# Splitting four fused weight products on GpSimd in place of VectorE, between ScalarE's eviction and the output product

## What is computed

```python
q = (hidden_states @ Wq).reshape(B, Sq, H, D)
k = (encoder_hidden_states @ Wk).reshape(B, Skv, H, D)
v = (encoder_hidden_states @ Wv).reshape(B, Skv, H, D)
q = rmsnorm(q, gq)
k = rmsnorm(k, gk)
scores = jnp.einsum('bqhd,bkhd->bhqk', q, k) * scale
attn = jax.nn.softmax(scores, axis=-1)
out = jnp.einsum('bhqk,bkhd->bqhd', attn, v)
return out.reshape(B, Sq, H * D) @ Wo
```

## Time and profile before

| | |
|---|---|
| median of three runs | 634.99 us |
| lowest and highest of them | 634.95, 635.37 us |
| span of the profiled execution, first to last instruction | 633.0 us |
| TensorE busy | 616.1 us, 97% of the span |
| VectorE busy | 489.0 us, 77% |
| ScalarE busy | 428.4 us, 68% |
| GpSimd busy | 231.0 us, 36% |

### The profile page before, as it was taken

How to read it: one execution, slowest core, us unless ns; L and a number is a source line. 1 busy time by engine, 2 the same in 40 slices (tenths; PEclk the granted TensorE clock), 3 DMA queues, 4 the chain that set the end, 5 groups by cost and what they waited for, 6 DMA issues and landing times.

```text
span 633.0 us, 11694 instructions
## 1 busy us (share of the span) xinstructions
PE 616.1 (97%) x3681; PEld 530.9 (84%) x3681; DVE 489.0 (77%) x1138; ACT 428.4 (68%) x1097; POOL 231.0 (36%) x275
## 2 busy tenths in 40 slices
PE   8888899999999999999999999999999999999997
PEld 5756678999999999999998888888887888887886
DVE  4999998777777678778867688788877777777776
ACT  5895999988888888879998544356444444444442
POOL 5677866766666666546664010000000000000000
PEclk9999999999999999999999999999999999999999
DMA  7420140100000000000012354444656466554640
GB/s 277 153 75 26 51 126 26 52 26 2 2 2 2 2 1 2 1 2 1 2 43 84 84 162 143 152 140 127 200 153 170 107 174 174 161 165 138 198 128 33
DMA packets 33509, 56.47 MB, mean 89 GB/s; under 512 B 12784, under 2 KB 13488, under 8 KB 33328
## 3 DMA queue, kind: packets, MB, share of 16 engines
q1 hardware_dynamic: 33456, 55.83, 29.3%
HBM read 53.45 MB, written 1.31 MB: 87 GB/s over the span
## 4 chain that ended last, share of the span: by engine, by line
PE 82%; DVE 8%; ACT 3%; issue 2%; POOL 2%; DMA 1%; SPq 0%; DVEq 0%; POOLq 0%; ACTq 0%
PE bank L286 24%; PE bank L288 23%; PE bank L287 23%; PE bank L834 4%; PE bank L809 2%; PE bank L801 2%; DVE w L1705 1%; DMA x<-in_x_tok 1%; DVE stats L1658 1%; DVE amax L1762 1%; POOL att L540 1%; ACT att L1341 1%; PE bank L716 1%; PE bank L868 1%; DVE w L1723 1%
## 5 line engine op out<-in xcount | busy, mean ns | idle before, releaser
L1380 ACT ACTIVATE inter_hi<-inter 128x512 fp32r<-128x512 f32 x63 | 39.8, 632 | 140.5 <-DVE inter L1940 140.5
L286 PE MATMUL bank<-xnT_hi,front_hi 128*128 128x512 f32 (+1 forms) x260 | 102.0, 392 | 0.0
L288 PE MATMUL bank<-xnT_hi,front_lo 128*128 128x512 f32 (+1 forms) x260 | 101.7, 391 | 0.0
L287 PE MATMUL bank<-xnT_lo,front_hi 128*128 128x512 f32 (+1 forms) x260 | 101.7, 391 | 0.0
L1944 DVE TENSOR_TENSOR inter_lo<-inter,inter_hi 128x512 fp32r<-128x512 f32 x63 | 43.6, 692 | 37.5 <-ACT inter_hi L1380 36.9
L1341 ACT ACTIVATE att<-bank,shift,rq 128x256 f32<-128x256 f32 x128 | 71.3, 571 | 0.0
L1829 DVE TENSOR_REDUCE rowmax<-bank 128x2 f32<-128x512 f32 x64 | 43.7, 685 | 27.4 <-PE bank L288 27.2
L540 POOL TENSOR_TENSOR att<-att,rowinv 128x512 f32<-128x512 f32 x60 | 62.1, 1054 | 5.2 <-DVE rowinv L1846 5.2
L524 POOL TENSOR_TENSOR rk<-msq,minus_half 128x4 f32<-128x4 f32 x32 | 33.1, 1035 | 78.7 <-DVE msq L1818 78.6
L1913 DVE TENSOR_TENSOR prod<-gate_s,bank 128x512 f32<-128x512 f32 x63 | 43.3, 687 | 21.9 <-PE bank L288 19.8
L287 PEld LDWEIGHTS bank<-xnT_lo,front_hi 128*128 128x128 f32 x260 | 48.9, 188 | 11.3
(11 more groups left out here) (273 smaller groups left out, 1843.3 us busy)
## 6 DMA issues: line engine op xcount, KB each, us to landing
w_all<-w_rows SPq DMA_DIRECT2D x128, 128.0 KB, 3.0
raw<-in_expert_w SPq DMA_DIRECT2D x32, 384.0 KB, 3.6
wvo_raw<-in_expert_w SPq DMA_DIRECT2D x16, 384.0 KB, 3.7
e_more<-in_expert_w SPq DMA_DIRECT2D x16, 384.0 KB, 3.6
raw<-in_head_qk SPq DMA_DIRECT2D x8, 384.0 KB, 3.6
wvo_raw<-in_head_vo SPq DMA_DIRECT2D x8, 384.0 KB, 3.2
gate_raw<-in_gate_wT SPq DMA_DIRECT2D x1, 1408.0 KB, 9.8
x<-in_x_tok SPq DMA_DIRECT2D x2, 512.0 KB, 6.1
```

The source lines that it names most:

```text
L286: pe.matmul(out, l_hi, r_hi_, start=start, stop=False, skip_group_check=True)
L287: pe.matmul(out, l_hi, r_lo_, start=False, stop=False, skip_group_check=True)
L288: return pe.matmul(out, l_lo, r_hi_, start=False, stop=stop, skip_group_check=True)
L1380: act.activation(inter_hi[:, slot, :], inter[:, slot, :], ACT.Copy).then_inc(a_Ihi, 1)
```

## The change

Head pairs 4 to 7 (`SPLIT = 4`) are treated another way. ScalarE's `whole_m(p)` scales the bank into `m_raw`, unrounded, at the place in its order where `high_m(p)` stood; `m_raw` shares its memory with `m_lo`. VectorE's four calls of `low_m` are gone. GpSimd's new `split_m(p)` stands in loop group g = p, behind `rms_q`: one instruction rounds `m_raw` into `m_hi`, GpSimd waits for it, and a second one writes the remainder over `m_raw`. TensorE's `output` waits for these pairs on the new count `g_Mlo`; the waits that protected the banks are now on `a_Mhi`, ScalarE's count.

```diff
@@ -29,6 +29,7 @@
 MAGIC = 12582912.0
 LOWEST = -3.0e38
 EARLY = 5
+SPLIT = 4
 LAST = 28
 GAIN = 127.0 / EPS
 
@@ -216,6 +217,11 @@
         back_hi = sc("back_hi", [P, PAIRS - EARLY, 768], F32R)
         back_lo = sc("back_lo", [P, PAIRS - EARLY, 768], F32R)
         cctx.close()
+        ectx = ExitStack()
+        ectx.enter_context(nc.sbuf_tensor("ahead_of_m", [P, 8704], F32))
+        m_whole = ectx.enter_context(nc.sbuf_tensor("m_whole", [P, PAIRS, 2, 2, HID], F32))
+        ectx.close()
+        m_raw = m_whole[:, :, 1, :, :]
         m_hi, m_lo = m_all[:, :, 0, :, :], m_all[:, :, 1, :, :]
 
         t_S, t_T, t_O, t_Y, t_Q, t_K, t_TQ, t_TK, t_M = (sem(n) for n in (
@@ -225,7 +231,8 @@
         v_max, v_shift_c, v_Tlo, v_Y, v_inv, v_Qlo, v_Klo, v_sqK, v_mk, v_mq, v_Olo, v_Mlo, v_gk = (
             sem(n) for n in ("v_max", "v_shift_c", "v_Tlo", "v_Y", "v_inv", "v_Qlo", "v_Klo", "v_sqK", "v_mk",
                              "v_mq", "v_Olo", "v_Mlo", "v_gk"))
-        g_rk, g_rq, g_kn, g_att, v_Wlo, g_Wlo = (sem(n) for n in ("g_rk", "g_rq", "g_kn", "g_att", "v_Wlo", "g_Wlo"))
+        g_rk, g_rq, g_kn, g_att, v_Wlo, g_Wlo, g_Mlo = (sem(n) for n in (
+            "g_rk", "g_rq", "g_kn", "g_att", "v_Wlo", "g_Wlo", "g_Mlo"))
 
 
         dctx = ExitStack()
@@ -539,6 +546,13 @@
                 a = att[:, n % 2, h, :, :]
                 pool.tensor_tensor(a, a, rowinv[:, n % 2, h, :].unsqueeze(2).broadcast_to([P, 2, SEQ]),
                                    ALU.mult).then_inc(g_att, 1)
+
+            def split_m(p):
+
+                pool.wait_ge(a_Mhi, p + 1)
+                link_g(pool, pool.tensor_scalar(m_hi[:, p, :, :], m_raw[:, p, :, :], 1.0, 0.0, ALU.mult, ALU.add))
+                pool.tensor_tensor(m_lo[:, p, :, :], m_raw[:, p, :, :], f(m_hi[:, p, :, :]),
+                                   ALU.subtract).then_inc(g_Mlo, 1)
 
             pool.wait_ge(pool_const, 5)
             pool.wait_ge(a_ctx, 1)
@@ -624,6 +638,8 @@
                     low_w(EARLY + 1, 2 * g)
                     pool.wait_ge(v_shift_c, g + 3)
                     low_w(EARLY + 1 + g, 1 - g)
+                if SPLIT <= g < PAIRS:
+                    split_m(g)
                 if g == 9:
                     pool.wait_ge(a_rw, 1)
                     pool.memset(f(r_both[:, 4 * LOGC:]), 0.0).then_inc(g_rw, 1)
@@ -851,7 +867,7 @@
                 b, p = g // PAIRS, g % PAIRS
                 pe.wait_ge(v_Olo, g + 1)
                 if b == 0:
-                    pe.wait_ge(v_Mlo, p + 1)
+                    pe.wait_ge(*((v_Mlo, p + 1) if p < SPLIT else (g_Mlo, p - SPLIT + 1)))
                 if p == 0 and h == 0:
                     wait(pe, v_Y, b)
 
@@ -1052,7 +1068,7 @@
             down(6, 7)
             down(7, 2)
             fuse_vo(6, 4)
-            pe.wait_ge(v_Mlo, 5)
+            pe.wait_ge(a_Mhi, 5)
             turn_rows_1(1, 5)
             pe.wait_ge(v_xB, 7)
             turn_q(1, 7)
@@ -1061,9 +1077,9 @@
             proj_q(3, 2, True)
             pe.wait_ge(c_u, 2)
             turn_rows_1(2, 5)
-            pe.wait_ge(v_Mlo, 6)
+            pe.wait_ge(a_Mhi, 6)
             fuse_vo(7, 6)
-            pe.wait_ge(v_Mlo, 7)
+            pe.wait_ge(a_Mhi, 7)
             turn_rows_1(3, 4)
             pe.wait_ge(v_Qlo, 2)
             proj_k(3, 7, True)
@@ -1073,7 +1089,7 @@
                 if g + 1 < GROUPS:
                     scores(g + 1)
                 if g == 0:
-                    pe.wait_ge(v_Mlo, 8)
+                    pe.wait_ge(a_Mhi, 8)
                 if g + 2 < GROUPS:
                     pe.wait_ge(a_sqQ, 4 * min(n, GROUPS))
                     turn_q(g + 2)
@@ -1351,6 +1367,11 @@
             def high_m(p, bk=KBK):
                 act.wait_ge(t_M, p + 1)
                 act.activation(m_hi[:, p, :, :], bank4(bk), ACT.Copy, scale=tg[:, 1:2]).then_inc(a_Mhi, 1)
+
+            def whole_m(p, bk):
+
+                act.wait_ge(t_M, p + 1)
+                act.activation(m_raw[:, p, :, :], bank4(bk), ACT.Copy, scale=tg[:, 1:2]).then_inc(a_Mhi, 1)
 
             def weight_exps(half):
                 act.wait_ge(v_shift, half + 1)
@@ -1490,26 +1511,26 @@
             square_q(1, 3)
             copy_q2(5, 6, 0)
             raw_q(2, 4)
-            high_m(4, 5)
+            whole_m(4, 5)
             square_q(2, 4)
             split_w(4)
             normalise_1(1)
             copy_q2(6, 4, 7)
-            high_m(5, 6)
+            whole_m(5, 6)
             copy_q2(7, 3, 2)
             normalise_1(2)
             exps(0, 0)
             exps(0, 1)
             copy_rows(1, 1, 5)
             act.wait_ge(a_h1, 7)
-            high_m(6, 4)
+            whole_m(6, 4)
             high_q(1, 7)
             high_k(1, 3)
             normalise_1(3)
             copy_rows(2, 2, 5)
             raw_q(3, 2)
             act.wait_ge(a_h1, 8)
-            high_m(7, 6)
+            whole_m(7, 6)
             copy_rows(3, 3, 4)
             raw_k(3, 7)
             square_q(3, 2)
@@ -2059,7 +2080,6 @@
             mean_q(1)
             stats_2(5)
             low_w(3)
-            low_m(4, 5)
             row_max(0, 0)
             row_max(0, 1)
             row_shift(0)
@@ -2071,14 +2091,11 @@
             row_inverse(0, 0)
             row_inverse(0, 1)
             low_rows(1, 1, 5)
-            low_m(5, 6)
-            low_m(6, 4)
             low_q(1, 7)
             low_k(1, 3)
             mean_q(2)
             low_rows(2, 2, 5)
             low_rows(3, 3, 4)
-            low_m(7, 6)
 
             for g in range(GROUPS):
                 n = g + 4
```

## The result

Four runs of the changed kernel gave 641.95, 640.19, 640.96 and 642.06 us, a median of 641.46 us, against 634.97 us for the kernel before beside them: a ratio of 1.0101 (95% interval 1.0088 to 1.0113), 6.5 us slower. The forecast was 640.3 us with a range up to 643.8. The spans of the four runs are 640.2 (the profiled one), 638.4, 639.2 and 640.0 us; their mean granted clocks, in the same order, 0.997, 1.0, 1.0 and 0.997. The forecast span was 638.4 us. So two of the runs agree with it to 0.8 us, and two, at a lower clock, are 1.6 and 1.8 us above it.

A forecast was written before the change was run, and what follows sets the result against it. TensorE was taken to bound the kernel, busy throughout loop groups 5 to 8. Late splits add 5.35 us and removing `low_m` nothing: 634.99 + 5.35 = 640.3 us, range 637.0 to 643.8 us.

The forecast's parts named there:

- The four `low_m` at nothing: Before the loop: removing VectorE's four passes, 2.9 us, gains 0, covered by ScalarE's program ahead of `turn_q(2)`.
- One sign: At the loop's start: group 0's `turn_q(2)` should start at 98.0 us as before, released by ScalarE.
- rival (d): Loop start: VectorE sets it, so the removed `low_m` give back up to 2.9 us; not slower, 635.9 us; chance 0.05.
- GpSimd's prices: In `split_m` on GpSimd: rounding 512 columns takes 0.62 us and the remainder 1.28 us.
- the sum worked out from it, 4.7 us: Groups 5 to 8: total loss if the remainder took the skill's 1.07 us instead of 1.28; 4.7 instead of 5.35 us.
- The stalls and how they add up: TensorE ahead of `output(g - 1, 0)`, groups 5 to 8: idle about 2.2, 0.95, 1.25 and 0.95 us, 5.35 in all.
- The rule itself: Groups 5 to 8: TensorE's lateness is the larger of its old lateness and 2.2 us plus GpSimd's lateness.
- The lateness of GpSimd: Groups 5 to 7: GpSimd late by 0.95, 2.2 and 3.15 us, through row inverses (1.25 us slack) or `msq`.
- rival (a): Groups 5 to 8: only the first stall costs, GpSimd's idle time absorbing the rest; 2.2 us, 637.2 us; chance 0.08.
- (c): Groups 5 to 8: each group pays in full, 4 x 2.2 = 8.8 us, 643.8 us; chance 0.05.
- Rival (b): Loop: GpSimd's remainder holds VectorE's `row_shift(6)` 0.85 us; if this came back in every group, 641.2 us; chance 0.10.
- Rival (e): Loop stalls: TensorE's clock falls; one group at half clock costs up to 8.1 us more, 648.5 us; chance 0.02.

The follow-up runs named there:

- e5_early_ahead: Changed kernel with GpSimd's split one loop group earlier and ahead of `rms_q` instead of behind it: 634.52 us, ratio 1.0000 to the kernel before.
- e6_dve4: e5_early_ahead with VectorE instead of ScalarE moving the four banks whole, at the places of the removed `low_m`: 633.91 us, ratio 0.9989 to the kernel before.
- e2_ahead: Changed kernel with each split in its own group but ahead of `rms_q`: 637.66 us, ratio 1.0043 to the kernel before.
- e3_pair7: Changed kernel with `SPLIT = 7`, so only pair 7 is split by GpSimd, pairs 4 to 6 as before: 638.23 us, ratio 1.0051 to the kernel before.
- e11_changed: The changed kernel again, unedited, beside e10_busy in the third set: 640.28 us, ratio 1.0090 to the kernel before.
- e1_early: Changed kernel with the split one loop group earlier, still behind `rms_q`: 635.51 us, ratio 1.0010 to the kernel before.
- e8_changed: The changed kernel again, unedited, in the second set, for its clocks: 641.25 us, ratio 1.0101 to the kernel before.
- e4_busy: Changed kernel with eight unused 512-column products filling TensorE's first stall, first set: 640.54 us, ratio 1.0095 to the kernel before.
- e10_busy: Changed kernel with the same fill of the first stall as e4_busy, third set: 640.31 us, ratio 1.0092 to the kernel before.

## Why the prediction held, and where it did not

**The four `low_m` at nothing: right.** The distance from `fuse_vo(4)` to `turn_q(2)`, 20.04 to 20.08 us with and without them, shows it in the traces, and e5_early_ahead shows it in the time, 634.52 beside 634.43 us. One sign was not as I wrote: the profile puts the idle time ahead of `turn_q(2)` down to "issue", not to ScalarE. That ScalarE's program is the cover is borne out twice: its last square ends 0.1 us ahead of `turn_q(2)` before, after and in e6_dve4, though that start moves, and e6_dve4 starts the loop 0.8 us sooner by taking passes off ScalarE and giving them to VectorE. So rival (d) falls.

**GpSimd's prices: right.** 0.62 and 1.27 us for 0.62 and 1.28. The floor of the Trainium skill (GPSIMD Engine Reference, 2.1 Instruction dispatch), by which the second would have lasted 1.07 us, is kept: 1.27 us lies above it. But the sum worked out from it, 4.7 us, is farther from the 5.6 us measured at clock 1.0 than 5.35 is.

**The stalls and how they add up: right.** Forecast 2.2, 0.95, 1.25 and 0.95 us, 5.35 in all; measured as surpluses at clock 1.0 2.2, 1.1, 1.2 and 1.1, 5.6 in all. The rule itself was tried twice with other numbers: e2_ahead gave its alternating stalls, e3_pair7 its single one. The lateness of GpSimd in e11_changed, 1.0, 2.2 and 3.3 us, is that of the forecast too, wait by wait. So rival (a), only the first stall, and (c), 8.8 us, fall.

**Rival (b), the shared path: right as a fact, and nothing in this sum.** It holds `row_shift(6)` for 0.88 us, and the later stalls are nevertheless those of the forecast, since the row inverses come later still. It has a price where nothing else is late: 0.7 us in e1_early, none in e5_early_ahead.

**Rival (e), the clock: the step that failed.** The prediction set "The granted clock is 1.00, which is 2.4 GHz, in every stretch, and stayed there over an idle time of 1.65 us" against it, gave it a chance of 0.02, and priced one group at half the clock at up to 8.1 us. The stall of 2.0 us that the changed kernel makes lies beyond that row, and the sum holds the clock at nothing. Measured, the clock was at half for some 3 us in the profiled run, which cost 1.6 us and not 8.1. Of the 14 runs of the changed kernel in three sets 6 have a mean clock of 0.997. Their spans have a mean of 639.9 us, those of the other eight 638.3, where 638.4 was forecast; the two are 1.6 us apart. The median of 641.46 us, 1.2 us above the forecast, lies between a run at 0.997 (span 640.2) and one at 1.0 (span 639.2, the longest of the eight), so the clock accounts for a part of the 1.2 us and the spread of the runs for the rest. How near a median comes to the forecast depends on how many of its runs have the low clock: 2 of 4 in the first set, 3 of 5 in e8_changed (641.25), 1 of 5 in e11_changed, whose 640.28 us is the forecast itself.

What makes the clock fall is less well shown than that it falls. With e3_pair7, which has one such stall, it is 9 of 19 runs; with the stall filled it is 0 of 8 (e4_busy, e10_busy), a split that chance would give about once in 50 times if both had the same rate; for the kernel before, beside the experiments, 1 of 57. Set by set, as they ran side by side, it is 3 of 5 (e3_pair7) against 0 of 4 (e4_busy), and 1 of 5 (e11_changed) against 0 of 4 (e10_busy), which is thin. The counts speak for idle time as the cause and don't settle it; the medians of e10_busy and e11_changed do not show it. Only in the profiles can the place be seen: in the changed kernel's and in e8_changed's it lies behind the stall, while the profiled run of e2_ahead had its lower clock in the first 20 us (0.91), so a mean of 0.997 alone doesn't tell that a stall was behind it. The Trainium skill (TensorE: Matmul & The Clock Gate, Part 1) says that idle time returns the engine to 1.2 GHz. Two traces agree, with the addition that the same stall does so in one execution and not in the next (e11_changed); what decides between them stays open.

So the time went three ways, of which the first two are in the forecast: 5.6 us of late splits where 5.35 were forecast, nothing for the removal, and 1.6 us of clock in 6 of 14 executions.

## What to carry to other kernels

An engine that is idle for over a third of the time (GpSimd was busy for 20.2 of 32.65 us in groups 5 to 8 of the kernel before) has room only before the moment at which its result is wanted: ask when its consumer needs it, and put handed-over work early enough, here one round of the loop, and clear of the other engine's instructions with two SBUF inputs (634.52 us in place of 641.25). Work taken off an engine gains only where that engine's program fills the path: VectorE's four passes were worth nothing, ScalarE's four 0.5 us. A stall in a loop that is otherwise full costs its length, once more through each queue that inherits it with too little slack, and at times a slower clock behind it.

## What the runs showed that I had not expected

- Behind an idle time of 2.0 us TensorE's granted clock was 0.50 from 143 to 146 us in the changed kernel's profile (products of 256 columns started 0.21 us apart) and 1.00 throughout in e11_changed, which has the same stall. By the mean clock it fell in 6 of 14 executions.
- One VectorE instruction on 128 x 4 numbers lasted 0.88 us instead of 0.15, because GpSimd was in a pass over 128 x 512. With that pass placed one group earlier and ahead of `rms_q` instead of behind it, the time was 0.1 us above the kernel before (e5_early_ahead) in place of 0.7 us (e1_early).
- Taking four passes of 0.7 us off ScalarE moved the loop by 0.8 us only; 0.8 us more turned into a wait for GpSimd.
